# Decoder layer on one core: initial keys in a fifth block, and a new order of value products, cross scores and the last projection

## The reference, cut to what matters

```python
def attn(x, Wq, Wk, Wv, Wo, last_k_init, last_v_init):   # 16 heads of 16, window 64
    k_pad = concatenate([last_k, k], axis=1)             # 63 initial keys ahead of the sequence
    v_pad = concatenate([last_v, v], axis=1)
    idx = arange(l)[:, None] + arange(w)[None, :]
    scores = einsum('blhd,blwhd->blwh', q, k_pad[:, idx]) * dh ** (-0.5)
    out = einsum('blwh,blwhd->blhd', softmax(scores, axis=2), v_pad[:, idx])
    return out @ Wo.T
x = x + attn(layernorm(x), ...)
x = x + xattn(layernorm(x), ctx, ...)   # cross attention, 16 heads of 64, 77 keys per batch
x = x + ffn(layernorm(x), ...)          # shared MLP and top 2 of 8 experts, width 1024
```

## Time and profile before

| what | us |
|---|---|
| three runs | 733.72, 738.21, 739.32 (median 738.21) |
| profiled execution | 734.35 |
| its span | 732.6 |
| PE busy | 683.6 |
| DVE, ACT, POOL busy | 414.4, 433.1, 391.1 |

### The profile page before, as it was taken

How to read it: one execution, slowest core, us unless ns; L and a number is a source line. 1 busy time by engine, 2 the same in 40 slices (tenths; PEclk the granted TensorE clock), 3 DMA queues, 4 the chain that set the end, 5 groups by cost and what they waited for, 6 DMA issues and landing times.

```text
span 732.6 us, 17453 instructions
## 1 busy us (share of the span) xinstructions
PE 683.6 (93%) x5652; PEld 642.6 (88%) x5652; DVE 414.4 (57%) x1035; ACT 433.1 (59%) x1621; POOL 391.1 (53%) x394
## 2 busy tenths in 40 slices
PE   8998999899979988999997899999999999997987
PEld 8887788788759888999887899999999999997887
DVE  5766777677755778999955323332333323234644
ACT  4447778687876866777743654545363545443452
POOL 8215666566755548777747929995392000035530
PEclk9999999999998999999999999999999999999999
DMA  9466544444408970000411534555151111113320
GB/s 275 121 200 181 135 134 130 119 127 121 128 1 312 384 274 29 29 22 29 145 53 58 164 138 116 201 181 166 43 174 54 46 44 44 43 62 97 107 81 30
DMA packets 95187, 87.86 MB, mean 120 GB/s; under 512 B 31899, under 2 KB 86901, under 8 KB 95125
## 3 DMA queue, kind: packets, MB, share of 16 engines
q1 hardware_dynamic: 85749, 60.86, 27.3%
q0 software_dynamic: 7776, 26.09, 10.8%
q10 hardware_dynamic: 1600, 0.15, 0.2%
HBM read 49.84 MB, written 37.22 MB: 119 GB/s over the span
## 4 chain that ended last, share of the span: by engine, by line
PE 65%; DVE 13%; issue 6%; SPq 5%; POOL 3%; ACT 2%; DMA 1%; another core or an unknown queue 1%; DVEq 0%; POOLq 0%; ACTq 0%
PE PQ L278 14%; PE PQ L280 14%; PE PQ L279 14%; SPq L428 4%; PE PQ L907 4%; PE PQ L848 3%; PE PQ L895 2%; PE PQ L923 2%; PE PQ L828 2%; PE PQ L1106 2%; DVE hot L1825 2%; PE PQ L1108 2%; PE PQ L1107 2%; POOL prob L566 2%; PE PQ L888 2%
## 5 line engine op out<-in xcount | busy, mean ns | idle before, releaser
L1491 DVE TENSOR_TENSOR htl<-PQ,hth 128x512 fp32r<-128x512 f32 x112 | 74.6, 689 | 140.4 <-ACT hth L1210 130.6
L1452 ACT ACTIVATE PQ<-PQ,b_all 128x256 f32<-128x256 f32 x160 | 65.1, 444 | 114.7 <-PE PQ L280 110.3
L278 PE MATMUL PQ<-wts,hth 128*128 128x256 f32 x448 | 128.4, 287 | 4.2 <-issue 3.0
L280 PE MATMUL PQ<-wts,htl 128*128 128x256 f32 x448 | 127.2, 284 | 1.6 <-issue 1.6
L279 PE MATMUL PQ<-wts,hth 128*128 128x256 f32 x448 | 126.5, 282 | 1.2 <-issue 1.1
L566 POOL TENSOR_TENSOR prob<-prob,rden 128x512 f32<-128x512 f32 x64 | 67.2, 1049 | 54.5 <-DVE rden L1622 52.8
L1375 ACT ACTIVATE prob<-PQ,negm 128x77 f32<-128x77 f32 x240 | 74.6, 365 | 35.4 <-DVE negm L1790 35.4
L1289 ACT ACTIVATE prob<-PQ,negm 128x128 f32<-128x128 f32 x256 | 90.9, 386 | 4.8 <-DVE negm L1616 2.6
L278 PE MATMUL PQ<-fxh,wts 128*128 128x256 f32 x320 | 90.6, 283 | 1.6 <-DVE fxl L1491 1.6
L278 PEld LDWEIGHTS PQ<-wts,hth 128*128 128x128 f32 x448 | 85.3, 190 | 6.6 <-issue 6.1
L280 PE MATMUL PQ<-fxh,wts 128*128 128x256 f32 x320 | 90.6, 283 | 0.0
(11 more groups left out here) (242 smaller groups left out, 2004.4 us busy)
## 6 DMA issues: line engine op xcount, KB each, us to landing
slots<-zeros SPq DMA_DIRECT2D x16, 1024.0 KB, 10.3
raw<-in_L_ffn_exp_w_dram POOLq DMA_DIRECT2D x16, 1024.0 KB, 5.9
Q<-turned_q SPq DMA_DIRECT2D x96, 64.0 KB, 2.4
K<-turned_k SPq DMA_DIRECT2D x48, 128.0 KB, 2.5
xf_sb<-slots SPq DMA_DIRECT2D x22, 256.0 KB, 2.6
slots<-y_sb SPq DMA_DIRECT2D x20, 256.0 KB, 2.1
turned_q<-flat_q SPq DMA_DIRECT2D x32, 128.0 KB, 2.4
turned_k<-flat_k SPq DMA_DIRECT2D x8, 512.0 KB, 3.2
```

Of the source, the lines that this page charges most:

```text
L278: pe.matmul(o, lh, rh, start=start, stop=False)
L280: return pe.matmul(o, ll, rh, start=False, stop=stop)
L1452: nc.scalar.activation(half, half, ACT.Gelu, bias=b1_all[:, at:at + 1]).then_inc(f["act"], 1)
L1491: return dve.tensor_tensor(o, whole, high.bitcast(F32), ALU.subtract)
```

## The change

K gets a fifth block, in which ACT and DVE put the initial keys at the start; kinit, `first_keys` and the semaphore a_k0 go, and the scores of tiles 0 and 8 read blocks 0 and 4. For the room, R1 grows by 448 bytes and xn2 and cT move. On PE `values(i // 2, 0)` stands ahead of `transposed` at s = 0 of even iterations. The projection of the last tile leaves iteration 18 and stands in cross(3), behind the second bank of scores of tile 1. In iteration 17 ACT splits tile 1 ahead of `evens` and takes the second bank of tile 0's exponentials behind it, and DVE subtracts ahead of `gathered`. In cross(3) DVE takes the first inverse sums behind the first peak, and the addition of the last tile behind the second.

```diff
@@ buffers @@
+    xn2 = Region(nc, keep.at, keep.end).place("xn2", [P, D], F32)
...
-    R1 = 48 * 1024
+    R1 = 48 * 1024 + 448
...
-    kinit = reg.place("kinit", [3 * PR, PAIRS, W], F32R)
     vinit = reg.place("vinit", [P, D], F32)
+    reg = Region(nc, reg.at + 4 * D, top)
...
-    K = idle.place("K", [3 * PR, PAIRS, 4, HB], F32R)
+    K = idle.place("K", [3 * PR, PAIRS, 5, HB], F32R)
...
+    cT = Region(nc, reg.at, top).place("cT", [CH, 2, B * CK], F32)
...
-    a_k0 = sem("a_k0")
@@ SP, keys_in @@
             if t:
                 sp.wait_ge(a["S"], C + 4 * (t - 1) + 2)
             else:
-                sp.wait_ge(a_k0, 1)
+                sp.wait_ge(p_pe, CH_VW)
@@ PE, scores @@
                 pe.wait_ge(k_in[q], 48 * (t // 2 + 1))
-                if t % TB == 0:
-                    pe.wait_ge(a_k0, t // TB + 1)
...
-                    blocks = K[:, p, 1:3, :] if q else K[:, p, 0:4:3, :]
+                    prev = 4 if t % TB == 0 else 3
+                    blocks = K[:, p, 1:3, :] if q else K[:, p, 0:prev + 1:prev, :]
@@ PE, self_attention @@
                 if i == NT + 1 and s == 0:
                     first_scores(2)
+                if has_values and s == 0:
+                    values(i // 2, 0)
                 if 0 <= n - 2 < 4 * NT:
                     transposed(n - 2)
...
-                if has_values and s == 0:
-                    values(i // 2, 0)
-                if s == 1 and is_tile(t - 2):
+                if s == 1 and is_tile(t - 2) and t - 2 < NT - 1:
                     projected_out(t - 2)
@@ PE, cross, in the loop over the three banks @@
                     last.then_inc(c["S"], 1)
+                    if type(i) is int and i == EARLY and k == 1:
+                        projected_out(NT - 1)
@@ ACT @@
-        copy(kinit[:, 0:4, :], PQ[BANK_OF[CH_KI]][0:3 * PR, 0, 0:4 * W].rearrange("p (a w) -> p a w", a=4)).then_inc(p_act, 1)
+        copy(K[:, 0:4, 4, :], PQ[BANK_OF[CH_KI]][0:3 * PR, 0, 0:4 * W].rearrange("p (a w) -> p a w", a=4)).then_inc(p_act, 1)
...
             if i == NT + 1:
-                first_exponentials(1)
+                early_high(1, cross_x)
             if i == NT - 1:
                 early_high(0, first_x)
             if is_tile(t - 1):
                 evens(t - 1)
             if i == NT + 1:
+                first_exponentials(1)
                 first_exponentials(2)
-                early_high(1, cross_x)
@@ DVE @@
-        dve.tensor_copy(kinit[:, 4:8, :], PQ[BANK_OF[CH_KI]][0:3 * PR, 1, 0:4 * W].rearrange("p (a w) -> p a w", a=4)).then_inc(p_dve, 1)
+        dve.tensor_copy(K[:, 4:8, 4, :], PQ[BANK_OF[CH_KI]][0:3 * PR, 1, 0:4 * W].rearrange("p (a w) -> p a w", a=4)).then_inc(p_dve, 1)
...
-        def first_keys(t):
-            if t:
-                dve.wait_ge(a["S"], C + 4 * t)
-                dve.wait_ge(k_in[1], 48 * (t // 2))
-            dve.tensor_copy(K[:, :, 3, :], kinit[:, :, :]).then_inc(a_k0, 1)
...
-            if is_tile(t - 2):
+            if is_tile(t - 2) and t - 2 < NT - 1:
                 added(t - 2)
...
+            if i == NT + 1:
+                early_low(1, cross_x)
             if is_tile(t - 1):
                 gathered(t - 1)
...
-            if i == NT + 1:
-                early_low(1, cross_x)
...
-            if not odd and is_tile(i) and i % TB == 0:
-                first_keys(i)
...
-        dve.wait_ge(p_pe, CH_VW)
-        first_keys(0)
         values_low(0)
...
-        dve.wait_ge(c["exp"], C + 3)
-        dve.reciprocal(den2[:, 1, :], den2[:, 0, :]).then_inc(c["rd"], 1)
-        early_normalized(2).then_inc(c["xn"], 1)
-        dve.wait_ge(a["x1"], C + NT)
-        dve.wait_ge(ld["small"], 48)
+        def last_tile_added():
+            added(NT - 1)
+            dve.wait_ge(a["x1"], C + NT)
+            dve.wait_ge(ld["small"], 48)
+            dve.memset(cum[0][:, :], 0.0)
+            for m in sums:
+                dve.memset(m[:, 0:E], 0.0)
+
+        def first_inverse_sums():
+            dve.wait_ge(c["exp"], C + 3)
+            dve.reciprocal(den2[:, 1, :], den2[:, 0, :]).then_inc(c["rd"], 1)
+            early_normalized(2).then_inc(c["xn"], 1)
@@ DVE, cross @@
+            if i == 6:
+                dve.wait_ge(rt_idx, 3)
...
             peak(0)
+            if i == EARLY:
+                first_inverse_sums()
...
             peak(1)
+            if i == EARLY:
+                last_tile_added()
...
-        dve.memset(cum[0][:, :], 0.0)
-        for m in sums:
-            dve.memset(m[:, 0:E], 0.0)
-        dve.wait_ge(rt_idx, 3)
```

More of the change, by code:

```diff
@@ L195, in decoder_layer @@
     xk_sb = reg.place("xk_sb", [CH, 2, XA], F32)
-    cT = reg.place("cT", [CH, 2, B * CK], F32)
     ctx_sb = reg.place("ctx_sb", [CK, B, CD], F32)
@@ L206, in decoder_layer @@
     xt2l = reg.place("xt2l", [P, DC, P], F32R)
-    xn2 = reg.place("xn2", [P, D], F32)
     XN3c = reg.place("XN3c", [P, D], F32)
```

## The result

| | us |
|---|---|
| before, four runs | 733.72, 735.43, 738.21, 739.32 (median 736.82) |
| after, four runs | 723.99, 725.22, 728.56, 729.24 (median 726.89) |
| ratio | 0.9869, 95% interval 0.9834 to 0.9903 |
| profiled execution after | 728.56, span 726.8 (before 734.35, 732.6) |

A forecast was written before the change was run, and what follows sets the result against it. TensorE (PE) was busy for 93% of the span, so only its idle or low-clock time could be won: 2.5 + 0.9 + 0.3 = 3.7 us off 736.3 gave 732.6 us, range 728.8 to 738.5.

The forecast's parts named there:

- the part on the cross scores: Last projection behind tile 1's second cross scores: 0.3 us won; moved memset and rt_idx wait, and other buffer moves, counted nothing.
- The sum of the order: All three reordered parts together: 2.5 + 0.9 + 0.3 = 3.7 us off the time.
- Keys in a fifth block: At tile 8's first scores, dropping DVE's copy wins 1.0 us of wait and 1.52 us of low clock, together 2.5 us.
- Values ahead: First steps of seven even iterations: value products fill PE's wait for POOL; 0.9 us won, bounds 3.6 won, 2.1 lost.
- Last projection: End of self-attention: cross scores fill PE's idle hole, the last addition comes 0.3 us earlier; bounds 1.8 won, 1.4 lost.
- the forecast's middle case: End of self-attention: second bank waits for exponentials until about 218.1, then 1.33 and 0.80 us; addition ends about 221.1.
- Behind the clearing: Before the first scatter: POOL's wait grows from 5.8 to 7 or 8 us, the scatter coming 3.7 us earlier.
- (a): Tile 8: key transfer replaces the copy, low clock may return, values' gain swallowed; 1.3 us won, 735.0; chance 0.20.
- (b): Even iterations' first steps: transposes come late, 0.80 us at each of seven places; 2.8 us slower, 739.1; chance 0.07.
- (d): Low clock falls elsewhere, or x1 comes 1.4 us late; gains cancel, 736.3, no change; chance 0.06.
- (c): Waits at tile 8 and the values go entirely, x1 0.9 us earlier; 8.0 us won, 728.3; chance 0.12.

The follow-up runs named there:

- e2: Kernel after with the expert buffers from r3p on and the groups' from gxh on moved up 64 bytes, restoring before's distances to wts; ratio to before 0.9948.
- e9: Kernel after with the keys part undone: DVE again copies the initial keys (from block 4) into block 3, with a_k0; single run, 719.23 us.
- e17: Kernel after with gxh and gxl alone moved up 64 bytes, hth kept at 128 modulo 256 from wts; ratio to before 0.9842.
- e1: Kernel before with htl, xf_sb, fxh, fxl and y_sb moved up 64 bytes, order unchanged; ratio to before 1.0005.
- e8: Kernel before with the buffers from r3p on (htl, fxh, fxl) and gxh, gxl, hth all moved up 64 bytes; ratio to before 0.9985.
- e10: Kernel after with the value products put back behind the late transposes; single run, 718.68 us.
- e11: Kernel after with the end of self-attention as before: last projection ahead of tile 1's cross scores, last addition behind the reciprocal; single run, 714.46 us.
- e3: Kernel after with gxh, gxl and hth alone moved up 64 bytes; ratio to before 0.9860.
- e13: Kernel before with htl, xf_sb, fxh, fxl and y_sb moved up 192 bytes; ratio to before 0.9893.
- e15: Kernel after with every operand pair of the split products placed at stationary less moving 64 modulo 256; ratio to before 0.9850.
- e12: Kernel after with everything behind window moved up 64 bytes, the buffers from r3p on and hth each by another 64; ratio to before 0.9895.
- e4: Kernel before with the weights wts alone moved up 64 bytes; single run, 721.77 us.
- e16: Kernel before with htl, fx, gx and hth moved up 192 bytes, each standing to wts as in after modulo 256; ratio to before 0.9900.

## Why the prediction was right and wrong

**The step that failed** is in the part on the cross scores: "The other moves of buffers change no size of an instruction." The sizes indeed stayed. But the moves set the operands' distances anew, and the sum put the moves at nothing. The 960 matmuls of fx went from 119.9 to 113.7 ns, 6.0 us, and with those of hth and htl the 20 units became 7.1 us shorter in the profile, of which gx's 384 matmuls gave back up to 1.9 (5 ns each). Measured by itself this is 0.9900 or 7.3 us (4.1 to 10.6 by the interval), about twice the whole forecast, and the sum had no term for it. The range had none either: its lower end was the order at its best.

**The sum of the order** came out right: 3.7 us forecast, 3.8 measured with distances as before (e2, 2 to 6 by its interval). But it was right by luck, as a net of two misses: at the clearing the order had won 4.7 us, and about 1 us of it was lost again later.

- Keys in a fifth block: the forecast was 1.0 us of wait and 1.5 of clock. The mechanism holds: the scores start at the moment the keys land, with 0.70 us of wait (forecast 0.9) and a clock of 1.00, and the pair takes 19.93 us (forecast 20 to 20.7). Undone it costs 3.1 us at tiles 7 and 8. Of these 1.6 are wait (1.96 us in e9, 0.33 in e17) and 1.5 clock. The clock's part doesn't come in every execution: six of the eight profiles of before's order have the low stretch between 131 and 139 us, e1 and e8 don't, and there the pair takes 21.57 us instead of 23.1 to 24.6. The wait that stays was put at 0.9 and was 0.70 and 0.33: with that the term was some 0.5 us too small. (By the prediction's own estimate of 2.3 us for a load the wait would shrink by 2.7 - 2.3 = 0.4 us, not 0.3. The sum doesn't use it.)
- Values ahead: the forecast was a product 1.42 us behind the transposes and 0.3 us at four of six places, 0.9 in all. Measured are 1.38 us and 0.4 us at a pair that pays, and by e10 the part is worth 1.2 us. In the profile shown nothing is won where the next scores wait for keys (19.57 and 19.61), as the forecast had it. But that is one execution: in the other eight profiles of the whole order PE doesn't wait there, and from the first scores of tile 9 to those of tile 11 it is 19.2 us, against 19.6 in all of before's order.
- Last projection: the forecast was 0.3 us, between 1.8 won and 1.4 lost. Measured are 0.6 us at its place and 0.7 for the stage. The second bank starts 2.85 us behind the last product (forecast 218.1 - 215.26 = 2.84), and the bank and the projection follow at the full clock, as the forecast's middle case had them. Only the rows on DVE ahead of the addition, for which that case left 0.45 us (221.1 less 218.1 + 1.33 + 0.80 + 0.42), cost next to nothing. In all eight profiles of before's order, and in e11, the clock is 0.50 somewhere between 214 and 228 us, in none with the seam of after.
- Behind the clearing: the forecast was a wait of POOL of 7 to 8 us and no loss. Measured are 10.00 us, since POOL was ready 8.9 us earlier (at 256.68 instead of 265.60) and the clearing 4.7. The prediction said that work won between 221 and 271 us is given back in that wait, but not that PE's longer idleness there costs clock afterwards. All nine profiles of the whole order have 3 to 10 us at 0.50 between 264 and 280 us; of before's order four of eight have 3 to 7, between 274 and 283. From the first self-attention scores to the last scatter the means are 342.5 and 345.9 us: of 4.5 us at the clearing 3.4 are left. That the seam is behind this loss is what e11 indicates, one profile against many: POOL waits 6.63 us in it, and 9.96 to 10.48 us in all eleven profiles with the seam.

**The rivals.** (a), (b) and (d) are refuted by these rows: no low clock in tile 8's pair, though the key transfer did take the copy's place as (a) says; turns not on the chain; x1 earlier. (c), all waits gone, gave 728.3 us, nearest to the 726.9 measured, but for a reason that didn't occur: PE still waits for keys at tile 8 and for DVE's copy at the values. A near number doesn't make the mechanism right. The Trainium skill's rule on short idles (TensorE: Matmul & The Clock Gate, "A second HAM failure mode"), which stood behind (a), did not bite: the trace has waits of 0.37 to 0.77 us at a clock of 1.00.

**What stays open** is the cause inside the chip. The Trainium skill, SBUF — State Buffer, section "Who interferes with whom", gives TensorE separate read ports for the moving operand and for the weight load, with nothing shared. By that rule the two reads would not hold each other up, at whatever distance they lie. The runs show that the distance counts: 119.9 against 113.7 ns. Through what part of the chip it does so isn't shown. The Trainium skill, TensorE: Matmul & The Clock Gate, section "Wait — 56ns, not 53.3ns?", has N / 2.4 GHz plus 2.5 ns, an estimate of 109 ns at 256 columns; no distance here reached it. Open too are why 64 gives 113 in some kernels and 118 in others (e3, e13, e15), depending on what runs ahead; why hth at 0 (e8 and e12, beside htl at 64) ran at 118 where fx and gx at 0 ran at 120; why after had units of 11.50 us in one execution and 11.64 in another; and whether the distance counts for matmuls of other shapes: K with Q, over 96 rows, with 128 columns and at distance 0, has 113 ns in before and after, but was not moved by itself.

## What to carry to other kernels

A diff that moves buffers is not neutral, even for stages whose code it leaves alone: list the addresses of both operands of every hot matmul, before and after, and take the spacing of their starts from the trace. Here fx at a distance of 0 modulo 256 from its weights was the slowest place, with either order, and shifting one region by 192 bytes (0.9893) won about twice as much as a rewritten order in three parts (0.9948). And before calling a gain the work of an edit, run the edit with the old places, and the new places with the old order.

## What the runs showed of the hardware

- The spacing of split fp32r matmuls (128x128 with 128x256) went with the distance of their operands' addresses: for fx 119.9 ns at 0 (gx 120 in e8), 113.7 or 117.8 at 64, 117.8 (113.4 in two of e1's twenty units) at 192, 118.6 on average at 128, 116.6 at 224. It didn't matter which of the two buffers was moved (e4 and e16 have the same units to the nanosecond). The distance alone doesn't settle the pace: at 64 fx had 113.7 ns in e17 and 117.8 in e15.
- The pace of one group of matmuls also hangs on how the group ahead of it is placed: with hth at 192 instead of 128 and all else alike (e3 and e17) every third unit takes 11.75 us, the others 11.34 and 11.55, instead of 11.50 for each.
- An idle stretch of PE of 6.40 us, from 265.0 to 271.4, came with a clock of 0.50 from 267.8 to 278.0 us, where before's stretch of 2.08 us had none. Waits up to 0.77 us between long rows of matmuls didn't lower it. In the kernels with before's order the wait of about 2 us ahead of tile 8 was followed by a low stretch in six of eight profiles and not in the other two.
